# Linear attention and a mixture of experts on one core: the down product of each expert taken half in rounded parts

## The reference

```
gx = xp[buf_tok]                                     # 64 experts x 128 rows x 512
gu = einsum('ech,ehi->eci', gx, gate_up_proj)        # 512 -> 384
g, u = split(gu, 2);  hid = silu(g) * u              # 192
eo = einsum('eci,eih->ech', hid, down_proj) * buf_w  # 192 -> 512
routed = zeros.at[buf_tok].add(eo)
```

## Time and profile before

| | us |
|---|---|
| median of 3 runs | 973.73 |
| lowest, highest | 968.06, 974.46 |
| profiled execution, its own time | 971.29 |
| its span | 969.4 |
| experts' stage in it | about 500 to 866 |
| mean granted TensorE clock, share of full speed | 0.989 |

### The profile page before, as it was taken

The page is one execution under the profiler, slowest core; times in us unless marked ns, Lnnn a source line. Parts: engine busy times, 40 slices in busy tenths (PEclk is TensorE's granted clock), DMA queues, the critical chain, the costliest instruction groups (busy, mean ns, idle before and its releaser), DMA issues. The chain is left out here.

```text
span 969.4 us, 15236 instructions
## 1 busy us (share of the span) xinstructions
PE 944.1 (97%) x4658; PEld 757.1 (78%) x4658; DVE 685.0 (71%) x1251; ACT 502.4 (52%) x1015; POOL 464.6 (48%) x543
## 2 busy tenths in 40 slices
PE   8999999999999999999999999999999999998996
PEld 7888888888888888877887777767777777767875
DVE  7977787969778796887766565655666665635776
ACT  5532444434343434534447565656565675534775
POOL 4002264555655555587234446454455554432564
PEclk9999999999999999989999999999999999999998
DMA  6343442434252433356558999999999999959963
GB/s 202 99 141 109 146 123 96 128 125 120 80 170 86 138 105 124 101 173 210 169 194 250 317 328 312 305 306 306 324 327 323 312 315 306 321 96 383 376 252 118
DMA packets 114191, 203.93 MB, mean 210 GB/s; under 512 B 18496, under 2 KB 56384, under 8 KB 113088
## 3 DMA queue, kind: packets, MB, share of 16 engines
q1 hardware_dynamic: 93584, 159.87, 49.5%
q0 software_dynamic: 19520, 35.75, 16.1%
q10 hardware_dynamic: 1008, 7.34, 2.0%
HBM read 143.03 MB, written 59.88 MB: 209 GB/s over the span
## 5 line engine op out<-in xcount | busy, mean ns | idle before, releaser
L1511 POOL DMA_INDIRECT slot_table<-tokens,slot_of x162 | 179.4, 1107 | 112.1 <-issue 59.7
L1553 POOL DMA_INDIRECT acc_rows<-eo,table_sb x64 | 111.0, 1734 | 172.7 <-ACT eo L879 138.3
L1608 PE MATMUL bank<-x_hi,wqkv_hi 128*128 128x512 f32 x384 | 153.4, 399 | 1.2 <-DVE wqkv_lo L963 1.1
L1608 PE MATMUL bank<-x_hi,wqkv_lo 128*128 128x512 f32 x384 | 150.7, 393 | 0.0
L1608 PE MATMUL bank<-x_lo,wqkv_hi 128*128 128x512 f32 x384 | 150.4, 392 | 0.0
L1376 DVE TENSOR_TENSOR wgu_lo<-wgu,wgu_hi 128x1536 fp32r<-128x1536 f32 x64 | 112.5, 1759 | 43.2 <-ACT wgu_hi L873 43.2
L1608 PE MATMUL bank<-wdn,hid_et 96*128 96x512 f32 x256 | 122.4, 600 | 6.2 <-ACT hid_et L915 6.1
L873 ACT CAST wgu_hi<-wgu 128x1536 fp32r<-128x1536 f32 x64 | 94.5, 1477 | 1.1 <-DMA wgu<-w_gu 0.5
L1542 POOL DMA_INDIRECT xg<-x_rows,table_sb x64 | 74.3, 1161 | 42.1 <-DVE table_sb L1111 22.8
L1608 PE MATMUL bank<-wgu_hi,xgt_hi 128*128 128x384 f32 x256 | 91.4, 357 | 0.0
L647 ACT ACTIVATE e<-bank 128x512 f32<-128x512 f32 x64 | 38.0, 593 | 97.4 <-PE bank L1608 97.4
(11 more groups left out here) (179 smaller groups left out, 2213.4 us busy)
## 6 DMA issues: line engine op xcount, KB each, us to landing
wgu<-w_gu SPq DMA_DIRECT2D x64, 768.0 KB, 8.1
wdn<-w_down SPq DMA_DIRECT2D x64, 384.0 KB, 8.3
xres<-x SPq DMA_DIRECT2D x32, 256.0 KB, 3.0
x_turned<-x1t SPq DMA_DIRECT2D x32, 256.0 KB, 2.7
x_rows<-x SPq DMA_DIRECT2D x32, 256.0 KB, 3.0
acc_rows<-x SPq DMA_DIRECT2D x32, 256.0 KB, 3.0
fin<-acc_rows SPq DMA_DIRECT2D x8, 1024.0 KB, 12.2
odd<-acc_rows SPq DMA_DIRECT2D x8, 1024.0 KB, 13.5
```

The source lines that it names most:

```text
L1511: pool.indirect_dma_start(table_dram, bass.IndirectOffsetOnAxis(slot_of[:, i, k:k + 1], 0), tokens[:, i:i + 1], None, bounds_check=SLOTS - ...
L1553: pool.indirect_dma_start(acc_dram[e % 2], bass.IndirectOffsetOnAxis(table_sb[:, e:e + 1], 0), eo[eo_slot[e]][:, :], None, bounds_check=T ...
L1608: mm = pe.matmul(out_ap, a, b, start=first and i == 0, stop=final and i == len(products) - 1)
```

## The change

A constant SPLIT = 1 says how many of the two halves of 96 rows are treated as high and low parts: the first one. ACT casts the first half of the down weights (`split_down`, 96x512) behind `scale_rows(e-1)`, for expert e+1; DVE subtracts, writing over the first half of the weight tile. ACT's copy of the turned hidden rows becomes two: the second half as it was, the first half as a cast. DVE subtracts that cast from PSUM (`split_hidden`), as the first thing of the next iteration. `down(e)` makes one fp32 product of the second half and three fp32r products of the first, and waits for both low parts. No buffer is added for loads; SP's and POOL's instructions are the same.

```
+            def split_down(e):
+                act.wait_ge(dn_in[e % ND], 16 * (e // ND + 1))
+                if e >= 2:
+                    act.wait_ge(eo_mm, e - 1)
+                act.copy(wdn_hi[e % 2][:, :, :], wdn_buf[e % ND][:, 0:SPLIT, :]).then_inc(wdn_hi_done, 1)
...
                 if e:
                     scale_rows(e - 1)
+                if e + 1 < NE:
+                    split_down(e + 1)
                 for _ in range(fills_of[e]):
                     unit()
                 act.wait_ge(ht_mm, e + 1)
                 if e >= 2:
                     act.wait_ge(eo_mm, e - 1)
-                act.copy(hid_et[e % 2][:, :, :], ht_ps[0:IH, 0:2 * P].rearrange("p (h s) -> p h s", h=2)).then_inc(hid_et_done, 1)
+                turned = ht_ps[0:IH, 0:2 * P].rearrange("p (h s) -> p h s", h=2)
+                if SPLIT < 2:
+                    act.copy(hid_et_rest[e % 2][:, :, :], turned[:, SPLIT:2, :])
+                act.copy(hid_et_hi[e % 2][:, :, :], turned[:, 0:SPLIT, :]).then_inc(hid_et_done, 1)
...
+            def split_down(e):
+                dve.wait_ge(wdn_hi_done, e + 1)
+                dve.tensor_tensor(wdn_lo[e % ND][:, :, :], wdn_buf[e % ND][:, 0:SPLIT, :], wdn_hi[e % 2][:, :, :].bitcast(F32),
+                                  ALU.subtract).then_inc(wdn_lo_done, 1)
+
+            def split_hidden(e):
+                dve.wait_ge(hid_et_done, e + 1)
+                if e >= 2:
+                    dve.wait_ge(eo_mm, e - 1)
+                turned = ht_ps[0:IH, 0:2 * P].rearrange("p (h s) -> p h s", h=2)
+                dve.tensor_tensor(hid_et_lo[e % 2][:, :, :], turned[:, 0:SPLIT, :], hid_et_hi[e % 2][:, :, :].bitcast(F32),
+                                  ALU.subtract).then_inc(hid_et_lo_done, 1)
...
             for e in range(NE):
                 ps = gu_ps[e % 2]
+                if e:
+                    split_hidden(e - 1)
...
                 if e + 2 < NE:
                     split_expert(e + 2)
+                if e + 1 < NE:
+                    split_down(e + 1)
...
             def down(e):
-                pe.wait_ge(hid_et_done, e + 1)
                 pe.wait_ge(dn_in[e % ND], 16 * (e // ND + 1))
                 if e:
                     pe.wait_ge(eo_done, e)
-                chain(eo_ps[:, :], [(hid_et[e % 2][:, k, :], wdn_buf[e % ND][:, k, :]) for k in range(2)]).then_inc(eo_mm, 1)
+                pe.wait_ge(wdn_lo_done, e + 1)
+                pe.wait_ge(hid_et_lo_done, e + 1)
+                products = [(hid_et_rest[e % 2][:, h - SPLIT, :], wdn_buf[e % ND][:, h, :]) for h in range(SPLIT, 2)]
+                for h in range(SPLIT):
+                    products += three(hid_et_hi[e % 2][:, h, :], hid_et_lo[e % 2][:, h, :], wdn_hi[e % 2][:, h, :], wdn_lo[e % ND][:, h, :])
+                chain(eo_ps[:, :], products).then_inc(eo_mm, 1)
```

More of the change, by code:

```diff
@@ L89, in build @@
     wgu_buf = [both.place(f"wgu{i}", [P, KC, GU]) for i in range(2)]
+    wdn_at = [both.at + 4 * i * 2 * D for i in range(2)]
     wdn_buf = [both.place(f"wdn{i}", [IH, 2, D]) for i in range(2)]
+    SPLIT = 1
     att = Map(nc, both.at, end)
@@ L192, in build @@
     wgu_lo = [Map(nc, at, at + 4 * KC * GU).place(f"wgu_lo{i}", [P, KC, GU], F32R) for i, at in enumerate(wgu_at)]
+    wdn_at += [late.at + 4 * i * 2 * D for i in range(ND - 2)]
     wdn_buf += [late.place(f"wdn{i}", [IH, 2, D]) for i in range(2, ND)]
+    wdn_lo = [Map(nc, at, at + 4 * SPLIT * D).place(f"wdn_lo{i}", [IH, SPLIT, D], F32R) for i, at in enumerate(wdn_at)]
     assert late.at <= projected_end + 8 * 4 * BT
@@ L206, in build @@
     hid_e = [late.place(f"hid_e{i}", [P, I]) for i in range(2)]
-    hid_et = [late.place(f"hid_et{i}", [IH, 2, P]) for i in range(2)]
+    hid_et_hi = [late.place(f"hid_et_hi{i}", [IH, SPLIT, P], F32R) for i in range(2)]
+    hid_et_rest = [late.place(f"hid_et_rest{i}", [IH, 2 - SPLIT, P]) for i in range(2)] if SPLIT < 2 else []
     assert late.at <= kept_from
@@ L212, in build @@
     xg += [late.place(f"xg{i}", [P, D + E]) for i in range(NXG - 2, NXG)]
+    wdn_hi = [late.place(f"wdn_hi{i}", [IH, SPLIT, D], F32R) for i in range(2)]
+    hid_et_lo = [late.place(f"hid_et_lo{i}", [IH, SPLIT, P], F32R) for i in range(2)]
     fin_map = Map(nc, both.at - 2 * 4 * (KC * GU + 2 * D), both.at)
@@ L358, in build @@
             sem("xgt_hi_done"), sem("wgu_hi_done"), sem("tanh_e_done"), sem("hid_et_done"), sem("eo_done"))
+        wdn_hi_done, wdn_lo_done, hid_et_lo_done = sem("wdn_hi_done"), sem("wdn_lo_done"), sem("hid_et_lo_done")
         stage_lo, x_lo_first, decay_done = sem("stage_lo"), sem("x_lo_first"), sem("decay_done")
@@ L896, in _ @@
             split_rows(0)
+            split_down(0)
             for _ in range(BEFORE_EXPERTS[2]):
@@ L1413, in _ @@
                     split_expert(e + 2)
+                if e + 1 < NE:
+                    split_down(e + 1)
                 for _ in range(fills_of[e]):
                     unit()
+            split_hidden(NE - 1)
             added = 0
@@ L1881, in _ @@
                 if e:
-                    pe.wait_ge(hid_et_done, e)
+                    pe.wait_ge(hid_et_lo_done, e)
                 for k in range(2):
```

## The result

| | before | after |
|---|---|---|
| median of 4 runs | 974.10 | 999.38 |
| lowest, highest | 968.06, 978.88 | 994.52, 1002.56 |
| profiled execution, its own time | 971.29 | 998.63 |
| its span; mean granted clock | 969.4; 0.989 | 996.9; 0.983 |

The ratio after by before is 1.0257, with an interval from 1.0224 to 1.0291: slower by 25 us, where I had forecast slower by 11. The sign and the kind of wait came as forecast, the size did not.

The account below looks back on a forecast made before the run. PE's own instructions were taken to set the pace, with the DMA engines also full. Waiting for down weights +17 (PE's gain deducted) and vanished waits -6 gave +11 on 971.3, 982.5; against the runs' median 985 us, range 969 to 1010.

Parts of the forecast that it names:

- kind of wait: ACT's cast of the down weights waits for their DMA, tens of us in all, absent before.
- Step 1: PE's down product falls from 1.72 to 1.54 us, gaining 0.18 an expert, 11.5 us in all.
- Rival D: Fp32r products of 96 rows no faster than a 0.43 us pass: +27 us, about 1001; chance 0.04.
- Step 2: ACT's added cast and split copy cost 0.76 us an expert; the work alone fits, with 0.3 left.
- Step 3: DVE's two added subtractions make a pair of experts without a unit 9.34 us instead of 8.95: +4 us.
- Step 4: ACT needs the down weights two experts after issue; at landing time 6.5 us this costs 0.87 a stretch, +17 us.
- L + 3.5: Least us from down(e-3) to down(e-1), L being the down weights' issue-to-landing time; L above 5.45 stalls a pair.
- rival C: Down weights' landing time stays at 8.5 us, a price of sharing, not backlog: about 1025; chance 0.15.
- Step 5: PE's present 6.1 us of waits, from late additions before ACT's copy, fall away: -6 us.
- A: Down weights land in time and DVE's chain decides: 971 to 976; chance 0.27.
- B: PE's gain stands whole, DVE's low parts being ready in time: 960, against the runs 962; chance 0.06.
- point of failure: Forecast wrong in its main step if ACT's wait for down weights stays under 5 us in all.

Follow-up runs that it names:

- e5: Changed kernel with PE's waits for the low parts moved behind the fp32 product of the second half: 988.27 us, ratio 1.0151.
- e6: Changed kernel with down weights of expert e, not e+1, treated in iteration e, and PE's low-part waits behind the fp32 product: 971.38 us, ratio 0.9980.
- e2: Changed kernel with cast and subtraction of the down weights of expert e instead of e+1 in iteration e: 985.70 us, ratio 1.0114.
- e3: Changed kernel with four down-weight buffers instead of three, each load issued one expert earlier: 984.03 us, ratio 1.0130.
- e11: e8 with only the first half of the down weights loaded from expert 3 on: 954.57 us, ratio 0.9790.
- e4: Changed kernel with only the first quarter of each 1 MB load of turned rows for blocks 3 to 7: 984.58 us, ratio 1.0124.
- e8: e6 with a fourth tile for the scaled rows: 978.13 us, ratio 1.0028.
- e12: Kernel before the change with a fourth tile for the scaled rows, all loads whole: 975.09 us, ratio 0.9998.

## Why the prediction was right or wrong

**Step 1, PE: right.** 1.55 us against 1.54; 10.5 us in all at full clock against 11.5. Rival D, rounded products as slow as an fp32 pass, falls with the 0.23 between them.

**Step 2, ACT: right.** The cast took 0.62, the two copies 0.26 each, for which I had 0.25; no wait traces back to ACT's work alone.

**Step 3, DVE: right.** 0.69 and 0.28; the pair at 9.27 to 9.31 against 9.34. Placing PE's wait later took off 11 us with the landing wait in place (e5) and 14 (985.70 - 971.38) without it (e6), but it shortens other waits by up to 0.9 us each as well, so these are upper ends. The waits that are DVE's alone add up to 10.5 us in the kernel after. I had priced a stage in which DVE decides every pair at +4 net, the gain already deducted, which is 15.5 gross (4 + 11.5); it decided eight pairs of 19.

**Step 4, the load of the down weights: the right mechanism, and the term that failed.** The law L + 3.5 held to a tenth, and e2 and e3 took the wait away by different means. The step that failed is the price: the single value of L, 6.5, for all 20 stretches. It would have made 28.5 us of waiting in the new kernel (17 net, plus the 11.5 of step 1). The trace has 39.7. L did fall, from 8.5 to a median of 7.0, so rival C is out. With 7.0 in its place the same sum gives +27 - 6 and a forecast of 995, so it looks as if half a microsecond of the median were all; the pairs show otherwise. In eight of the 19 pairs without a unit L was 5.8 or less and DVE's order decided. In nine L was 6.3 to 7.2. These 17 have 21.7 us of waiting, where the sum had 24. The other two, with L of 10.4 and 11.1, have 11.2 us, where it had 2.8, and some 7 us more stand outside such pairs, where it had hardly any, 3.1 of them right behind the third 1 MB load, issued at 702.46. Landings of 9 to 11 us behind the 1 MB loads thus made most of what was missing. In the kernel before, the step from a median of 6.3 to 10.5 begins right behind the first of the 1 MB loads, issued at 553.35; I read all of it as backlog of PE's pace, which a slower kernel would shed, and averaged. (Part of it may be: L went on rising to 12.7 at 616, long after that load.) In the kernel after, such a load is issued three times in the stage, whatever PE's pace, and the down weights issued next land late. "DMA: Bandwidth & Descriptors" of the Trainium skill, section Issuing engines are not separate DMA queues, says that transfers started by different engines run on the same 16 DMA engines and interleave; the trace agrees, since the 1 MB goes through ACT's queue and the late weights through SP's, 10.4 and 11.7 us from issue to landing.

**The half clock: not in the sum at all.** +4.8 us. "TensorE: Matmul & The Clock Gate" of the Trainium skill, section HAM oscillation, describes a kernel whose PE comes back throttled from each wait for a DMA; the trace agrees at the two long waits, 0.54 in 571 to 576 and 0.50 in 857 to 860. A third place, 767 to 770 with a clock of 0.61, followed a wait of only 1.53 us, and in the kernel before 635 to 638 with 0.69 followed one of 1.89, while a wait of 1.74 at 719 was followed by full clock. So the waits of 4.46 and 5.08 us cost the clock both times, and shorter ones did or didn't. With the 10 us of waiting beyond what the sum had (32.6 more than before, against 28.5 - 6) and 1 us less of gain, the 4.8 make up the miss: +27.3 measured in the profiled executions, +11 forecast.

**Step 5: right in kind.** The old waits for additions did go, 34.7 to 7.6 on ACT. They came back in e2 (24.8) and e6 (34.7) as soon as the wait that covered them was taken away.

**Rivals.** A (weights in time) is out: 38.6 us of waiting. (The formula of the Trainium skill, "DMA: Bandwidth & Descriptors", section Anatomy of one DMA, is for one transfer started by GpSimd; these are started by SP, many at a time, and took 3.6 us at least.) B (faster) is out for this kernel; in e11, with other waits and fewer bytes, its gain shows. The forecast's point of failure, under 5 us of waiting on ACT, was not touched.

**What stays open.** Whether the 1 MB loads, cut into pieces and spread over the stage with all their bytes, would save what e4 saved by leaving bytes out was not tried. What makes the landings at those places 8 to 10 us long even behind quarter loads is not known either. Nor is it shown what decides the clock after the shorter waits.

## What to carry to other kernels

Before a load's first use is moved forward, follow the buffer's whole loop (last read, issue, landing, first use, the work queued behind that) and hold it against the distance of the iterations, with the longest landing times and the large loads that cause them, not with the median. Look at the share of the DMA engines before work is taken off another engine: where they were full here, a faster PE was paid back in waits (e6, e8). Whether one more buffer helps has to be tried: one for the loads that PE's path waited for took off 15 us (e3), one for the additions only moved the wait to another transfer (e12). Put a wait behind whatever does not depend on it: doing that on ACT and on PE (e6) took back 28 us that no arithmetic was changed for.

## What the runs showed of the hardware

- After a wait of PE of 4.46 us the granted clock was 0.54 in the next 5 us and 0.78 in the 5 after that, with fp32r products of 512 columns 0.43 apart, then 0.23 again.
- A fourth buffer for the additions raised the landing time of unrelated 384 KB loads from a median of 8.5 to 13.1 us, with the engines at 305 GB/s in 510 to 860 in both kernels (e12 and the one before). The loads came no faster, only later.
- An fp32r product of 96 rows took the 0.23 us of one of 128 rows: fewer rows bought nothing.
